# Second layer of an fp32 kernel: 32x32 turns on VectorE in place of 128x128 turns on TensorE, the last sum in pairs and on GpSimd

## The reference, cut to what matters

```python
x = x + ffn0(cond0(x))            # layer 0: 128x128 matrix per batch, then 2048 x 2048
x = x + ffn1(conv1(x))            # layer 1

def conv1(x, c, weight, c_weight, bias):      # 4 groups of 32 channels, 9 taps, pad 4
    out = lax.conv_general_dilated(x, weight, (1,), [(4, 4)], feature_group_count=4)
    return out + (c @ c_weight.T)[:, :, None] + bias[None, :, None]

def ffn1(x, up, down, perm):                  # x as rows of 2048
    t = x.reshape(b * l, 2048)[:, perm].reshape(b * l, 16, 128)
    t = gelu(einsum('bhd,hdm->bhm', t, up))   # 128 -> 512
    t = einsum('bhm,hmd->bhd', t, down)       # 512 -> 128
    return t.reshape(b * l, 2048)[:, argsort(perm)]
```

## Time and profile before

| | |
|---|---|
| median of 3 runs | 2580.77 us (2577.89 to 2582.27) |
| the profiled execution's own time | 2583.87 us |
| its span in the trace | 2582.0 us |
| TensorE matmul busy | 2528.0 us, 98% |
| VectorE busy | 1822.8 us, 71% |
| ScalarE busy | 1001.8 us, 39% |
| GpSimd busy | 950.8 us, 37% |
| DMA, mean over the span | 210 GB/s |

### The profile page before, as it was taken

How to read it: one execution, slowest core, us unless ns; L and a number is a source line. 1 busy time by engine, 2 the same in 40 slices (tenths; PEclk the granted TensorE clock), 3 DMA queues, 4 the chain that set the end, 5 groups by cost and what they waited for, 6 DMA issues and landing times.

```text
span 2582.0 us, 39106 instructions
## 1 busy us (share of the span) xinstructions
PE 2528.0 (98%) x12090; PEld 2099.3 (81%) x12090; DVE 1822.8 (71%) x2667; ACT 1001.8 (39%) x1632; POOL 950.8 (37%) x826
## 2 busy tenths in 40 slices
PE   8899999999999999999999999999999999999997
PEld 6788888888888888888888778888888888888775
DVE  6665555965556755576445768888888888888876
ACT  3221212321122322232222555555555555555573
POOL 2366645466654455233223212222222222222231
PEclk9999999999999999999999999999999999999998
DMA  9965644665545777576555754577767676777786
GB/s 318 322 196 199 201 168 155 238 210 197 196 163 185 228 229 228 161 250 210 160 165 186 223 153 131 170 219 219 221 214 226 205 223 205 225 226 223 212 281 240
DMA packets 417281, 541.02 MB, mean 210 GB/s; under 512 B 36248, under 2 KB 270064, under 8 KB 417072
## 3 DMA queue, kind: packets, MB, share of 16 engines
q1 hardware_dynamic: 314816, 307.40, 39.6%
q10 hardware_dynamic: 78144, 154.27, 15.9%
q0 software_dynamic: 24112, 76.80, 9.4%
HBM read 309.72 MB, written 228.61 MB: 208 GB/s over the span
## 4 chain that ended last, share of the span: by engine, by line
PE 91%; DVE 4%; DMA 2%; issue 2%; ACT 1%; ACTq 0%; SPq 0%; POOL 0%; DVEq 0%; POOLq 0%
PE ps_c L461 44%; PE ps_up L1398 13%; PE ps_y L1408 13%; PE ps_c L1423 9%; PE ps_v L439 4%; PE ps_c L427 2%; PE ps_zt L1436 2%; PE ps_f L1444 2%; DVE w_lo L1004 1%; PE ps_up L1423 1%; DVE ring_lo L951 0%; DVE r_early L1000 0%; DMA a_s<-in_lora_a 0%; DMA x_n<-in_up 0%; DMA aggw_d<-agg 0%
## 5 line engine op out<-in xcount | busy, mean ns | idle before, releaser
L461 PE MATMUL ps_c<-w_hi,ring_hi 128*128 128x512 f32 x1792 | 703.8, 393 | 3.8 <-DVE r_early L1000 3.2
L461 PE MATMUL ps_c<-w_hi,ring_lo 128*128 128x512 f32 x1792 | 698.0, 390 | 0.0
L461 PE MATMUL ps_c<-w_lo,ring_hi 128*128 128x512 f32 x1792 | 697.8, 389 | 0.0
L611 ACT ACTIVATE ring_hi<-raw_n 128x512 fp32r<-128x512 f32 x382 | 239.4, 631 | 848.7 <-DVE raw_n L942 235.1
L1380 POOL DMA_INDIRECT y_d<-y_s,idx x128 | 145.7, 1139 | 723.1 <-ACT y_s L1548 689.6
L1505 ACT ACTIVATE kern<-ps_up 128x512 f32<-128x512 f32 x512 | 306.6, 599 | 257.5 <-PE ps_up L1398 245.4
L461 PEld LDWEIGHTS ps_c<-w_hi,ring_hi 128*128 128x128 f32 x1792 | 336.7, 188 | 74.5 <-issue 4.0
L461 PEld LDWEIGHTS ps_c<-w_hi,ring_lo 128*128 128x128 f32 x1792 | 336.4, 188 | 70.2
L461 PEld LDWEIGHTS ps_c<-w_lo,ring_hi 128*128 128x128 f32 x1792 | 336.7, 188 | 67.3
L1622 DVE TENSOR_TENSOR g_lo<-kern,g_hi 128x512 fp32r<-128x512 f32 x512 | 354.5, 692 | 38.2 <-ACT g_hi L1509 21.8
L1000 DVE TENSOR_TENSOR r_early<-ps_c,r_early 128x512 f32<-128x512 f32 x256 | 176.6, 690 | 276.2 <-PE ps_c L461 276.2
(11 more groups left out here) (211 smaller groups left out, 3832.9 us busy)
## 6 DMA issues: line engine op xcount, KB each, us to landing
u_d<-raw_n ACTq DMA_DIRECT2D x64, 512.0 KB, 3.2
x_d<-r_early ACTq DMA_DIRECT2D x128, 256.0 KB, 3.6
raw_n<-u_d SPq DMA_DIRECT2D x64, 512.0 KB, 3.6
x_d<-x_s ACTq DMA_DIRECT2D x126, 256.0 KB, 2.7
u_s<-x_d SPq DMA_DIRECT2D x496, 64.0 KB, 2.2
z_d<-x_s SPq DMA_DIRECT2D x120, 256.0 KB
rear<-y_d SPq DMA_DIRECT2D x112, 256.0 KB
rear<-x_d SPq DMA_DIRECT2D x112, 256.0 KB, 4.0
```

Source lines behind the costliest of these rows:

```text
L461: mm = nc.tensor.matmul(bank, a[:, dc, :], w[k][:, dc, :], start=(first and dc == 0 and n == 0), stop=(dc == 3 and n == 2), skip_group_che ...
L611: nc.scalar.activation(ring_hi[g % RING][:].rearrange("p a n -> p (a n)"), factor(q, k, p), ACT.Copy).then_inc(hi_ready, 1)
```

## The change

- Both turns go to VectorE, as transposes of 32x32 blocks. `turn_z` is one instruction per unit, from `z_s` (now two buffers) to `zt`; the rest of the turn is made by how SyncE writes `z_d` (`z_rows`). TensorE's eight transposes per step and VectorE's copy from `ps_zt` go.
- The order of the convolution units within a block becomes group by group, batches inside (`conv_unit`).
- The final work is made for two steps at once (128x1024): `load_rows` (4 DMAs), `load_final_x1`, `turn_y` (one transpose by VectorE), `add_x1` (GpSimd, new), `store_out`. The output is written in phase order and put in place after the kernel returns, outside the device time.
- `split_t` and `gather` go one step further ahead (2 and 3); `t_hi`, `t_lo` and the bank of `ps_y` are doubled.
- ScalarE makes two of the four casts to `g_hi` in every step, not in the late ones only.
- The second buffer of the lead (`second`) no longer lies over `g_hi` and `g_lo`, and SyncE's wait for the last stores of layer 0 moves from ahead of the stream to unit 16.
- The last 16 units: contiguous operands, 64 stores of 64 KB by SyncE and ScalarE in place of 16 of 256 KB by ScalarE.

```diff
-                    sh.load_group(sp, x1_d, sh.xp[t - 4], t - 4, 0, t - 4)
+                    sh.load_group(sp, x1_d, sh.xp[t - 4], t - 4, t - 4, 0)
...
-        ps_c, ps_zt, ps_y, ps_f = bank("ps_c"), bank("ps_zt"), bank("ps_y"), bank("ps_f")
+        ps_c, ps_last = bank("ps_c"), bank("ps_last")
+        ps_y = [bank(f"ps_y{j}") for j in range(2)]
...
-        def by_scalar(k, h, mc):
-
-            return late(k, h) and mc % 2 == 1
+        def by_scalar(mc):
+
+            return mc % 2 == 0
...
+            group, batch = divmod((h + LEAD) % H, SB)
+            return H * k + h + LEAD, h % 2, SB * k + SB * ((h + LEAD) // H) + batch, group
...
-                sp.dma_start(yt_s[j], y_d[1 - parity][c * 512:(c + 1) * 512, h // 4 * C:(h // 4 + 1) * C]
-                             .rearrange("(l p) r -> p l r", p=P)).then_inc(yt_in[j], 16)
-                wait(sp, o_ready, v - 1)
-                sp.dma_start(x1_s[j], x1_d[b, :, :, c * P:(c + 1) * P]).then_inc(x1_in[j], 16)
+                wait(sp, fin_done, pair(k, h))
+                rows = y_d[1 - parity].rearrange("(q w i s) n -> q s i w n", q=2, w=8, s=S)[w % 2, w // 2]
+                for g in range(G):
+                    sp.dma_start(yt_s[g * GC:(g + 1) * GC, :].rearrange("p (w n) -> p w n", w=8),
+                                 rows[:, :, g * C:(g + 1) * C]).then_inc(yt_in, 16)
+
+            def load_final_x1(k, h):
+
+                wait(sp, o_out, 16 * pair(k, h))
+                sp.dma_start(x1_s.rearrange("p (b q) -> p b q", b=SB), final_part(x1_d, k, h // 2)).then_inc(x1_in, 16)
...
+            def add_x1(k, h):
+                pool.wait_ge(fin_done, pair(k, h) + 1)
+                pool.wait_ge(x1_in, 16 * (pair(k, h) + 1))
+                nc.gpsimd.tensor_tensor(x1_s, o_s, x1_s, ALU.add).then_inc(o_ready, 1)
...
-                for w in range(4):
-                    mm = nc.tensor.transpose(ps_zt[:, 0, w * P:(w + 1) * P], z[:, w * P:(w + 1) * P], id_s[:])
-                mm.then_inc(zt_done, 1)
...
-                for l in range(4):
-                    mm = nc.tensor.transpose(ps_f[:, 0, l * P:(l + 1) * P], yt_s[j][:, l, :], id_s[:])
-                mm.then_inc(fin_done, 1)
...
-                nc.vector.tensor_copy(zt_of(k, h)[:, :, :, g * GC:(g + 1) * GC],
-                                      ps_zt[:, 0, :].rearrange("p (w r o) -> p w r o", w=4, r=S)).then_inc(zt_ready, 1)
...
-                nc.vector.tensor_tensor(o_s[j].rearrange("p (q s) -> p q s", s=S),
-                                        ps_f[:, 0, :].rearrange("p (q s) -> p q s", s=S),
-                                        x1_s[j].rearrange("p s q -> p q s"), ALU.add).then_inc(o_ready, 1)
+                nc.vector.transpose(zt_of(k, h)[:, :, n % SB, :], z_s[h % 2][:]
+                                    .rearrange("p (w c) -> p w c", w=WIDE)).then_inc(zt_ready, 1)
+
+            def turn_y(k, h):
+                dve.wait_ge(yt_in, 64 * (pair(k, h) + 1))
+                wait(dve, o_ready, pair(k, h))
+                nc.vector.transpose(o_s.rearrange("p (b w i) -> p b w i", b=SB, w=8),
+                                    yt_s.rearrange("p (w b c) -> p b w c", w=8, b=SB)).then_inc(fin_done, 1)
...
-            for p in range(2):
-                for blk in range(4):
-                    sp.wait_ge(sh.r_out[p][blk], 16 * QUADS)
             drive(sp, step)
```

More of the change, by code:

```diff
@@ L27 @@
 XP_ROOM = 640
+WIDE = Q // GC
+Y_LO = 576
 def wait(eng, sem, value):
@@ L1250, in load_x1, with load_rows @@
                 wait(sp, xlo_ready, u - 3 if isinstance(u, int) and u < H + 2 else u - 1)
+                if isinstance(u, int) and u == H:
+                    for p in range(2):
+                        for blk in range(4):
+                            sp.wait_ge(sh.r_out[p][blk], 16 * QUADS)
                 j = xp_of(k, h)
                 sh.load_group(sp, x1_d, xp[j], j, b, g)
-            def load_final(k, h, parity):
-                v, j, b, c = final_unit(k, h)
+            def load_rows(k, h, parity):
+                w = h // 2
                 if h == 0:
@@ L1308, in step @@
                     load_x1(*after(*after(k, h)))
-                if exists(k, h, LEAD - 2) and (h + LEAD - 2) % G == G - 1:
-                    store_z(k, h, parity)
-                if not lead(k) and exists(k, h, LEAD + 2):
+                elif not lead(k) and exists(k, h, LEAD + 2):
                     load_x1(*after(*after(k, h)))
@@ L1505, in gelu @@
                 nc.scalar.activation(g_s[:, mc, :], ps_up[:, mc, :], ACT.Gelu).then_inc(gelu_done, 1)
-                if by_scalar(k, h, mc):
+                if by_scalar(mc):
                     act.wait_ge(gelu_done, MC * s + mc + 1)
-                    act.wait_ge(down_done, MC * (s - 1) + mc + 1)
+                    wait(act, down_done, MC * (s - 1) + mc + 1)
                     nc.scalar.activation(g_hi[:, mc, :], g_s[:, mc, :], ACT.Copy).then_inc(ghi_scalar, 1)
             def step(k, h, parity):
-                if not lead(k) and exists(k, h, 1) and not early(*after(k, h)):
-                    split_t(*after(k, h))
+                if not lead(k) and exists(k, h, 2):
+                    split_t(*after(*after(k, h)))
                 if lead(k):
@@ L1529, in step @@
                         act.wait_ge(zt_ready, H)
-                        for w in range(2, 4):
-                            act.dma_start(z_d[0][w * 512:(w + 1) * 512, (SB - 1) * C:SB * C]
-                                          .rearrange("(q r) n -> q r n", r=S), zt_pair[1][:, w, :, :]).then_inc(z_out[1], 16)
+                        for r in range(2, S):
+                            act.dma_start(z_rows(z_d[0], r, G - 1), zt_pair[1][r * GC:(r + 1) * GC].rearrange("p w b c -> p w (b c)")).then_inc(z_out[1], 16)
                     if not lead(k) and exists(k, h, LEAD + 1):
                         split_x(*after(k, h))
+                if lead(k) and exists(k, h, 2):
+                    split_t(*after(*after(k, h)))
                 if isinstance(k, int) and H * k + h == -1:
-                    nc.scalar.activation(y_s[1][:, 0:1], cbias[:, 0, 0:1], ACT.Gelu)
-                    split_t(0, 0)
+                    nc.scalar.activation(y_room[:, Y_LO + Q + 2:Y_LO + Q + 3], cbias[:, 0, 0:1], ACT.Gelu)
                     act.wait_ge(wsplit_lo, CHUNKS)
@@ L1541, in step @@
                         gelu(*after(k, h), mc)
-                if exists(k, h, 2) and early(*after(*after(k, h))):
-                    split_t(*after(*after(k, h)))
                 if exists(k, h, 0):
@@ L1631, in step @@
                         split_weights(n)
-                if exists(k, h, LEAD - 1):
-                    take_z(*before(k, h))
-                if final_exists(k, h, 1):
-                    take_final(*before(k, h))
+                if exists(k, h, LEAD):
+                    turn_z(k, h)
                 if not lead(k) and exists(k, h, LEAD + 1):
                     split_x(*after(k, h))
-                if isinstance(k, int) and H * k + h == -1:
-                    split_t(0, 0)
+                if lead(k) and exists(k, h, 2):
+                    split_t(*after(*after(k, h)))
+                if h % 2 == 1 and pair_exists(k, h):
+                    turn_y(k, h)
                 if exists(k, h, 1):
```

252 lines of the change are left out of this document (101 added, 151 removed).

## The result

The changed kernel takes **2516.25 us** (median of four executions, 2515.42 to 2517.59), the kernel before 2580.02 on the same chip: a ratio of 0.975, 95% interval 0.974 to 0.977. So 64 us were gained where I forecast 97. The profiled execution took 2516.26 us, with a span of 2514.4 and a mean granted clock of 0.989.

What follows compares the result with a forecast made beforehand. The prediction took TensorE as the bound, VectorE next in line. Its savings, 79 + 7 + 6 + 3 + 2 = 97 us, took 2583.9 to 2487; the median lies 3 us lower, so 2484 us, range 2467 to 2525.

Steps and rivals of the forecast that it cites:

- Points 1 to 4: Full steps and first block: without TensorE's turns a full step takes 7.57 us, saving 79 and 7 us; VectorE keeps up.
- point 4: Full steps: GpSimd's sum, behind `split_x`, delays `g_lo`, but 2 us remain before TensorE needs it; transfers cost nothing.
- The thin slack: Full steps: VectorE, with GpSimd's hold charged in full, needs 14.2 of 15.1 us for two steps, a slack of 0.9.
- Point 5: The 20 late steps, without convolution: VectorE is the bound at 5.9 us a step, saving 6 us (bounds 0 and 14).
- rival C: Full steps: one-buffer chain through SyncE (sum, store, x1 load, z store) delays `turn_z`; 2495 to 2530 us, chance 0.17.
- Point 6: The lead, 20 units before step 0: moving the wait for layer 0's last stores saves 3 us (bounds 0 and 9).
- Point 7: Last 16 units: contiguous sums, with more stores to issue, take 0.8 us a unit, saving 2 us (bounds 0 and 5).
- A: Full steps: transposes cost more than a copy and VectorE becomes the bound; 2523 or about 2560 us, chance 0.17.
- B: Full steps: 4-byte transposes run at a fraction of a copy's rate; some 215 us slower at four times, chance 0.06.
- as told: Whole kernel: the main forecast without any rival, a time of 2470 to 2496 us, chance 0.58.

## Why the forecast was right, and where it was wrong

**Points 1 to 4, right.** The full step is 7.56 us (7.57 forecast), the first block gained 7.3 us (7). The durations behind them were right to 0.02 us for both transposes, the sum lasts 2.4 (2.6 at most), the hold shows in full in the rows above, and no TensorE wait for `g_lo` shows in full steps. One detail of point 4 was wrong without harm: the sum does not start behind `split_x` but 0.04 us ahead of it, so it is mostly `xp_lo` that is held, and not `g_lo`. The guess that a transpose costs what a copy of the same 32-wide pieces costs carried most of the forecast. The thin slack was another than the one that I had counted: VectorE had some 1.6 us a pair to spare, and what gave way first, with the sum doubled or one place later, was the store of z.

**Point 5, wrong in sign** (6 forecast as gained, about 10 lost). "Here VectorE is the bound" is true only with `load_last_x1` out of the way: with these loads moved, the stretch was 123.4 us against the 124 that the point implies. I had not put their 4 MB into the walk at all; the windows that I read (2490 to 2540) began in the middle of them. I took the DMA engines from point 4: "220 GB/s become 245, against 253 already seen", a comparison of rates. What counts is how much of their time the bytes take. In full steps 220 GB/s took 71 or 72% of it before, and 242 take 85% now; with the 4 MB, 92% was 287 GB/s before, and 91% is 226 now. A byte costs more of their time than it did, by 7 to 9% in full steps (0.85 / 242 against 0.72 / 220 and 0.71 / 220) and by 26% there (0.91 / 226 against 0.92 / 287). The change had rewritten these loads so that each of them lands on 32 partitions instead of 128. That can be no more than part of the reason: with these loads out of the stretch a byte still costs 16% more than before (0.84 / 226 against 0.92 / 287). Why a byte costs more stays open; no run here keeps the new order with the old shape of the loads, and z's stores and the loads of `y_d` and x1 changed their shapes as well.

Nor had their time quite run out at 91%. With the loads spread, or with the sum on VectorE, the same engines were busy for 97 and 99% and moved 250 and 246 GB/s. In the changed kernel's chain, the dear bytes of the four loads lie ahead of x1's load, and everything else waits for the round trip; that this leaves the engines their 9% of idle time is my reading, and was not tested by itself.

The other condition of the loss is GpSimd's sum, 8 to 12 us with the 4 MB in place, and nothing without them (123.4 us with the sum on GpSimd); the pair's chain of sum, store and x1 load took 16.7 us there. I had named that round trip in rival C and placed it in full steps, where it kept pace (7.56). It failed in the late ones, where the load takes 10 us, and not for want of a buffer.

**Point 6, wrong in sign** (3 forecast, 6 lost, with scatter of 3). The part that I had seen is there: the first load behind layer 0 comes at 1458.6 in the mean of the ten profiles (1456.3 to 1461.2) instead of 1462.38 and 1461.80, some 3.5 us earlier (3.0 forecast). But from that load to step 0 it now takes 68.7 to 73.0 us instead of 61.4 and 61.0. "SyncE's queue is busy without a gap" was a property of the old order, in which z was stored two units behind its turn, and I carried it over without asking where the store stands now. The dearer issue of the stores, 2.4 us for the first three groups of four, was missing as well. The granted clock went the same way. How the 9.5 us divide between these stays open.

**Point 7, wrong in sign, by little** (2 forecast, 3 lost). The units do come faster: from the first sum to the end of the last it is 11.2 us (15.3 before), better than the 0.8 us a unit that I took. But VectorE's last sum is no longer what ends:

```profile
2503.87 1.28 DVE L1614 TENSOR_TENSOR rear<-ps_up,w_lo 128x512 f32<-128x512 f32 x2
```
```profile
2504.97 4.82 SPq L1172 DMA_DIRECT2D out_dram<-kern  x8
2509.83 1.84 SPq L1172 DMA_DIRECT2D out_dram<-rear  x4
```

The 64 stores take 0.46 to 0.65 us each to issue (0.4 forecast), two a unit on each queue, so the queues are 6.5 to 7 us behind at the end; from the last sum to the end of the span it is 9.2 us instead of 4.1. I had the price of a store and the number of them, and looked at the rate of VectorE rather than that of the queues. Another 1.8 us come from the wait for the last rows, which land later.

**The rivals.** A did not occur (0.71 us). B did not either. C cost nothing in full steps, though its wait was there (6.3 us in 200), and is what happens when the sum is a little later (15 us in every fourth step), or twice as long (11.4). The range (2467 to 2525) held the time through C's allowance, by another mechanism than C: that is luck. The forecast "as told" (2470 to 2496) did not hold it.

## What to carry to other kernels

When a bound is shortened by 10%, walk not only the steady steps but each stretch in which extra transfers run, and work out how much of the DMA engines' time its bytes take rather than GB/s: what a byte costs of it is not constant (0.0032 to 0.0040 of their time per GB/s in these late steps). When an experiment makes the mean step longer, look at the steps one by one: a loss at every fourth step points to what is done once in four. If a row of a queue is "without a gap", ask which waits the change puts into that queue, and count the issues per unit on each queue against the engine that feeds them. A sum of two SBUF operands handed to GpSimd to spare VectorE cost VectorE 2.3 us here; doing it itself cost 1.2. And a queue in order makes a chain out of transfers that have nothing to do with each other: here the store of the last result holds up the store of z.

## What the runs showed of the hardware that I had not expected

A GpSimd sum of 1024 elements held up a subtraction with two inputs on VectorE for its whole 2.40 us, and the same sum on VectorE takes 1.22 us, so that the helper was dearer than the work. VectorE's 32x32 transposes in 4 bytes run at the rate of the copy from PSUM that they replaced (0.69 us), 0.71 us for 512 elements a partition and 1.23 for 1024, the latter read in permuted pieces. The DMA engines, busy for 91 and 92% of the time, moved 226 GB/s in one kernel and 287 in the other. And taking small work (0.44 us a unit) out of TensorE's stream in the lead went together with a lower granted clock, 0.97 and 1.00 before, 0.87 to 0.94 in ten profiles after; the stream has longer gaps now, and that these are the reason is not tested.
